# Finer pieces at the borders of stages, and in the running sums, of an eight-stage network on one core

## The reference

```python
S = jax.nn.relu(att[:, 0]); S = S.at[..., 0].set(0.0); S = S * (1.0 - eye)
FF = jnp.cumsum(shift_down_one_row(S), axis=1)       # running sum over the queries
att = att - FF[:, None]
keep = rank_of(FF_with_inf_above_diagonal) < eff_k   # about 409 keys per row, and the diagonal
y = softmax(where(keep, att, -inf)) @ v
```

## Time and profile before

| | |
|---|---|
| Time, 3 runs | 3022.83 us median (3011.96 to 3023.34) |
| The profiled execution | 3018.02 us, its span 3016.3 us, mean TensorE clock 0.946 |
| Busy, share of span | TensorE 88%, VectorE 63%, ScalarE 59%, GpSimd 11% |
| Running sums | 30.0 to 145.0 us |
| Attention of stage 1 | 400.3 to about 1010 us |
| Border 6 to 7: load issued, first product | 2755.97 and 2775.55 us |
| Border 7 to 8: output bias, first logit | 2825.15 and 2844.07 us |
| Load issued at the end, last instruction | 3001.87 and 3010.78 us |

### The profile page before, as it was taken

How to read it: one execution, slowest core, us unless ns; L and a number is a source line. 1 busy time by engine, 2 the same in 40 slices (tenths; PEclk the granted TensorE clock), 3 DMA queues, 4 the chain that set the end, 5 groups by cost and what they waited for, 6 DMA issues and landing times. The chain is left out here.

```text
span 3016.3 us, 75172 instructions
## 1 busy us (share of the span) xinstructions
PE 2657.2 (88%) x30828; PEld 1637.2 (54%) x30828; DVE 1889.0 (63%) x5219; ACT 1765.3 (59%) x3448; POOL 340.7 (11%) x709
## 2 busy tenths in 40 slices
PE   7898968888888799999998989999999999795386
PEld 3386955666666562212122546676666767463254
DVE  5399988878787573100001758878878787654762
ACT  2376846656666428999996246666666666421231
POOL 2100023222222010000000000000000000043025
PEclk9898989999999899999999999999999999897698
DMA  3250001111100102100000010000000000312003
GB/s 108 35 58 1 2 2 17 17 17 17 17 17 10 53 1 76 54 33 1 1 1 17 1 39 7 2 7 7 7 2 7 7 2 2 94 25 36 28 16 56
DMA packets 79982, 67.81 MB, mean 22 GB/s; under 512 B 40440, under 2 KB 67208, under 8 KB 79256
## 3 DMA queue, kind: packets, MB, share of 16 engines
q1 hardware_dynamic: 71192, 56.70, 8.1%
q0 software_dynamic: 8448, 6.30, 1.6%
HBM read 47.21 MB, written 19.96 MB: 22 GB/s over the span
## 5 line engine op out<-in xcount | busy, mean ns | idle before, releaser
L1711 ACT ACTIVATE arena<-ps 128x1024 f32<-128x1024 f32 x512 | 474.1, 1281 | 25.9 <-PE ps L1661 24.0
L1159 DVE CUSTOM_DVE_ANT_0 arena<-ps,arena 128x1024 f32<-128x1024 f32 (+7 forms) x384 | 350.1, 931 | 104.7 <-PE ps L1033 89.4
L2090 DVE CUSTOM_DVE_ANT_0 arena<-ps,arena 128x512 f32<-128x512 f32 (+3 forms) x640 | 373.0, 643 | 16.3 <-PE ps L1954 13.2
L1109 ACT ACTIVATE arena<-ps 128x1024 f32<-128x1024 f32 (+2 forms) x320 | 274.4, 895 | 125.0 <-PE ps L1066 121.5
L2044 ACT ACTIVATE arena<-arena 128x1152 f32<-128x1152 f32 (+15 forms) x256 | 306.0, 1200 | 60.2 <-DVE arena L2090 60.1
L1672 PE MATMUL ps<-arena 128*32 128x512 f32 x2048 | 273.0, 604 | 0.0
L1985 PE MATMUL ps<-arena 128*64 128x128 f32 x4352 | 268.8, 276 | 2.3 <-DVE arena L2105 1.5
L1954 PE MATMUL ps<-arena 64*128 64x512 f32 (+3 forms) x1280 | 266.0, 541 | 2.1 <-ACT arena L2020 1.1
L1985 PEld LDWEIGHTS ps<-arena 128*64 128x64 f32 x4352 | 234.7, 137 | 55.4 <-issue 45.7
L868 PE MATMUL ps<-arena 128*128 128x256 bf16 (+1 forms) x2176 | 238.1, 273 | 15.7 <-DVE arena L840 9.0
L1802 DVE COPY arena<-ps 128x512 f32<-128x512 f32 x16 | 11.1, 692 | 356.5 <-PE ps L1672 356.5
(11 more groups left out here) (294 smaller groups left out, 4159.6 us busy)
## 6 DMA issues: line engine op xcount, KB each, us to landing
arena<-scr_q SPq DMA_DIRECT2D x256, 32.0 KB
scr_s<-scr_f SPq DMA_DIRECT2D x1, 4096.0 KB, 16.9
arena<-scr_k SPq DMA_DIRECT2D x32, 128.0 KB
arena<-by_head_k SPq DMA_DIRECT2D x16, 192.0 KB
arena<-scr_s SPq DMA_DIRECT2D x16, 192.0 KB, 2.6
arena<-by_head_q SPq DMA_DIRECT2D x28, 96.0 KB
by_head_k<-arena SPq DMA_DIRECT2D x5, 512.0 KB, 4.4
scr_x<-arena SPq DMA_DIRECT2D x2, 1024.0 KB, 5.3
```

Source lines behind the costliest of these rows:

```text
L1109: e.activation(turned_block(u, kc), src, ACT.Exp, scale=-1.0).then_inc(exped, 1)
L1159: e.tensor_tensor_reduce(scored_block(u, g)[:, lo:hi], PS[:, 1024 * (k % 2):1024 * (k % 2) + hi - lo], NF[t][:, lo:hi], -1.0, mxs[:, col - ...
L1711: e.activation(PTR[k % RS], PS[:, at(n):at(n) + 1024], ACT.Sigmoid, scale=float(1 / np.sqrt(8.0))).then_inc(weighed, 1)
L2090: e.tensor_tensor_reduce(slot(u, t, g)[:, lo:hi], PS[:, base(step) + 512 * g:base(step) + 512 * g + hi - lo], bias, -1.0, mxs[:, col - 1:c ...
```

## The change

1. **Running sums.** Scores go two tiles ahead instead of one (a third `srow`), and piece by piece between the sums' pieces. The carry is added by pieces, right after each piece's sum, and a sum waits for its own piece's carry only. `cacc` is cleared by GpSimd at the start of the program. `X + bias`, `rpe_vector` and `split` move 2 or 3 tiles later. The third `srow` lies over `QS`, so SP's loads of queries wait for the last carry.
2. **Attention.** The first pair is (0, 7) instead of (7, 0). Three units of tile 0 go first, tile 7's penalty is made between them, and tile 0 stays three units ahead.
3. **Borders of stages 6, 7 and 8.** The reload of `X` goes in four DMAs with a semaphore each. In stage 6, `norm_moments` and `norm_rows` of stage 7's quarters 0 to 2 stand between the additions; in stage 7, likewise for stage 8. Stage 7's four output biases stand ahead of its additions. Logits come between the `norm_turn` of quarters. `wide(7)` and `weigh(7)` stand behind the last `down` and `scale`. The output goes in four DMAs.

```diff
+            order = [("score", n) for t in (0, 1) for n in pieces_of[t]]
+            for t in range(NT):
+                more = [("score", n) for n in pieces_of[t + 2]]
+                while len(more) > len(pieces_of[t]):
+                    order.append(more.pop(0))
+                for n in pieces_of[t]:
+                    if more:
+                        order.append(more.pop(0))
+                    order.append(("sum", n))
...
             def sums_scalar(e, w):
...
-                        if t >= 2:
-                            w.wait_ge(f_carry, t)
...
+                        if t >= 3:
+                            w.wait_ge(f_carry, upto[t - 3])
...
             def sums_vector(e, w):
-                e.memset(cacc, 0.0).then_inc(f_carry, 1)
-                for t in range(NT):
-                    W = 128 * (t + 1)
-                    w.wait_ge(f_summed, upto[t])
+                w.wait_ge(filled, 2)
+                for n, (t, c0, c1) in enumerate(chunks):
+                    w.wait_ge(f_summed, n + 1)
...
-            pairs = [(7, 0), (15, 1), (14, 2), (13, 3), (12, 4), (11, 5), (10, 6), (9, 8)]
+            pairs = [(0, 7), (15, 1), (14, 2), (13, 3), (12, 4), (11, 5), (10, 6), (9, 8)]
...
+            ahead = 3
+            units = [(0, p) for p in range(ahead)]
+            for p in range(8):
+                units += [(7, p)] + [(0, p + ahead)] * (p + ahead < 8)
+            units += [(t, p) for x in pairs[1:] for p in range(8) for t in x]
...
-                e.dma_start(by_tile(X), sum_rows.rearrange("(t p) c -> p t c", p=128)).then_inc(ec["d_back"], 16)
+                for c in range(4):
+                    e.dma_start(by_tile(cols(X, c)), sum_rows[512 * c:512 * c + 512].rearrange("(t p) c -> p t c", p=128)).then_inc(ec_back[c], 16)
...
                 for c in range(4):
+                    w.wait_ge(ec_back[c], 16 * (r + 1))
                     v = e.tensor_tensor(cols(X, c), cols(X, c), cols(SUM, c), ALU.add)
-                v.then_inc(x_ready, 1)
+                    if r == 0 and c < 3:
+                        norm_ahead(e, w, 6, c, 6, v)
+                        if c:
+                            norm_rows(e, w, 6, c - 1, ROWS7)
+                    elif r:
+                        v.then_inc(x_added, 1)
+                if r == 0:
+                    v.then_inc(x_ready, 1)
+                    norm_rows(e, w, 6, 2, ROWS7)
...
                     for c in range(4):
-                        w.wait_ge(ln_ht, 24 + max(c + 1, min(n, 3) + 1))
+                        if n == 3:
+                            norm_turn(e, w, 6, 3, HR, 3)
+                        w.wait_ge(ln_ht, 24 + c + 1)
...
-            e.dma_start(out.rearrange("b (t p) c -> p (b t) c", p=128), by_tile(X)).then_inc(d_out, 16)
-            w.wait_ge(d_out, 16)
+            for c in range(4):
+                w.wait_ge(x_added, 12 + c + 1)
+                e.dma_start(rows[:, 4 * c:4 * c + 4, :], by_tile(cols(X, c))).then_inc(d_out, 16)
+            w.wait_ge(d_out, 64)
```

More of the change, by code:

```diff
@@ L661, in qkv_vector @@
                 w.wait_ge(d_w, 64)
-                w.wait_ge(ones, 1)
+                w.wait_ge(filled, 1)
                 for n in range(12):
@@ L678, in qkv_gpsimd @@
             def qkv_gpsimd(e, w):
-                e.memset(V9, 1.0).then_inc(ones, 1)
+                e.memset(V9, 1.0).then_inc(filled, 1)
+                e.memset(cacc, 0.0).then_inc(filled, 1)
             cacc = reg(AT + 4096, 2048)
@@ L898, in stage1 @@
             extras = {}
+            for j in range(n_penalty[7]):
+                extras.setdefault((ahead * j // n_penalty[7], 1, 0), []).append((7, j))
             for k in range(1, 8):
@@ L901, in stage1 @@
                 for i, x in enumerate(steps):
-                    extras.setdefault((16 * (k - 1) + 15 * i // len(steps), 1, 0), []).append(x)
+                    first = ahead if k == 1 else 0
+                    extras.setdefault((16 * (k - 1) + first + (15 - first) * i // len(steps), 1, 0), []).append(x)
             plan = TileOrder(units, tiles, extras, space, {"score": -0.3, "shift": 0.1, "flip": -0.65, "add": -0.8, "turn": -0.15, "close": -0.3})
@@ L1136, in attend_vector @@
                 e.memset(SM[:, 256:320], 0.0).then_inc(fixed, 1)
-                for t in pairs[0]:
-                    for j in range(n_penalty[t]):
-                        penalty_vector(e, w, t, j)
+                penalty_vector(e, w, 0, 0)
                 for step in plan.steps:
@@ L1184, in attend_gpsimd @@
                 w.wait_ge(fixed, 6)
-                clear(e, w, pairs[0][0])
                 for step in plan.steps:
@@ L1232, in stage1 @@
             return {"sync": sync, "tensor": tensor, "vector": vector, "scalar": scalar, "gpsimd": gpsimd}
-        moe = {n: sem(f"m_{n}") for n in ("d_w", "logits", "scored", "routed", "made", "gated", "hidden", "spread", "turned", "scaled", "summed", "added")}
+        moe = {n: sem(f"m_{n}") for n in ("d_w", "logits", "scored", "routed", "made", "gated", "hidden", "spread", "turned", "scaled", "summed")}
         def stage_moe(r, stage, next_rows):
@@ L2290, in tensor @@
                         merge(x + 2)
-                    wide(x + 2)
+                    if x < 5:
+                        wide(x + 2)
                 down(5)
+                wide(7)
+                if r == 0:
+                    for c in range(3):
+                        norm_turn(e, w, 6, c, ROWS7, c)
             N_COPIED = 12
@@ L2561, in tensor @@
                     m.then_inc(mixed, 1)
+                for c in range(3):
+                    norm_turn(e, w, 7, c, ROWS8, 4 + c)
             def scalar(e, w):
                 w.wait_ge(x_ready, 6)
-                layernorm_scalar(e, w, 6)
+                norm_root(e, w, 6, 3)
+                norm_take(e, w, 6, 3, 3)
                 for i, m in enumerate((M, E)):
@@ L2617, in ended @@
         def ended(e, w):
-            w.wait_ge(x_ready, len(stages))
-            e.dma_start(out.rearrange("b (t p) c -> p (b t) c", p=128), by_tile(X)).then_inc(d_out, 16)
-            w.wait_ge(d_out, 16)
+            rows = out.rearrange("b (t p) c -> p (b t) c", p=128)
+            for c in range(4):
+                w.wait_ge(x_added, 12 + c + 1)
+                e.dma_start(rows[:, 4 * c:4 * c + 4, :], by_tile(cols(X, c))).then_inc(d_out, 16)
+            w.wait_ge(d_out, 64)
         block = ctx.enter_context(nc.Block())
```

130 lines of the change are left out of this document (77 added, 53 removed).

## The result

Median of 14 runs 3008.35 us (3000.14 to 3021.72), beside 3022.39 us (3011.8 to 3029.91) of the kernel before. The ratio is 0.9958, its 95% interval 0.9941 to 0.9975: 7.5 to 18 us gained, 12.7 in the middle. The forecast was 19.4 (3000 us). The profiled execution took 3005.58 us, its span 3003.8, which is 12.5 less than before.

The account below looks back on a forecast made before the run. TensorE was taken to bound the running sums, VectorE the attention's start, a DMA, VectorE and TensorE chain the borders. -10.8 - 2 + 1.3 - 2.7 - 1 - 4.2 = -19.4 on 3018.0 us: 2998.6, given as 3000; range 2987 to 3014.

Parts of the forecast that it names:

- Clock: Running sums: long 8-row score blocks lower TensorE's clock; with single pieces 16.9 us lost becomes 4.5, a gain of 12.4.
- The third rival: Running sums: single 8-row pieces between sums hold the clock at half through tiles 6 to 13; 3056 us, chance 0.06.
- Changes: Running sums: 63 instead of 29 changes between scores and sums on TensorE, 0.19 us each; 6.5 us lost.
- Idle: Running sums: TensorE's waits for the clear and carries shrink from 5 to 1.5 us, tile 3 still waiting; gain 3.5.
- Tail: After the last sum: only the last 512 columns' carry is left, some 0.7 us instead of 2.29; gain 1.4.
- Attention's start: First pair of the attention: tile 7's last three units run without a tile 0 unit and its wait; -2 us.
- Border 6|7: Stage 6 to 7: weights issued behind a later x_ready become the late wait, fourth norm_turn delays the fourth product; +1.3 us.
- Border 7|8: Stage 7 to 8: VectorE's layernorm ends 1.1 us earlier, two quarters of logits precede the last norm_turn; -2.7 us.
- 5|6: Stage 5 to 6: rows come no earlier, only the interleaving counts; -1 us.
- The end: Last reload of X and store of the output: load and store overlap by quarters; -4.2 us.
- the first rival: Running sums: the clock does not come back, its falls having another cause than score blocks; 3011 us, chance 0.25.
- this rule: Running sums: an always busy TensorE keeps its clock, so short scores bring nothing back; the sum lacks 12.4 us.

Follow-up runs that it names:

- e_before2: The kernel before, run once more with no edit: 3054.98 us, beside 3048.46 for the kernel before.
- e_oldsums: The changed kernel with the running sums of the kernel before (parts 2 and 3 of the change only): 3051.39 us, kernel before 3048.46.
- e_clear: The changed kernel, but GpSimd makes its clears without waiting for the constants at the start: 3002.63 us, kernel before 3013.88.
- e_oldatt: The changed kernel with the attention's old order, pair (7, 0) first and its penalties ahead of everything: 3009.34 us.
- e_wearly: The changed kernel, but SP loads stage 7's weights in the middle of stage 6, not after x_ready: 3036.50 us, kernel before 3048.46.
- e_wapart: The changed kernel, but stage 6's hidden products wait only for W1 and b1, not W2 and b2: 3029.89 us, kernel before 3048.46.
- f_after2: The changed kernel unchanged, run again on another chip: 3037.65 us (median of seven), ratio 0.9959 to the kernel before.
- e_blocks: The changed kernel, but all scores of a tile stand in one block ahead of a tile's sums: 3005.78 us, kernel before 3013.88.
- e_rows128: The kernel before, but its scores contract over all 128 rows instead of 8, so they sum all heads: 3002.29 us, kernel before 3013.88.
- f_zero: The changed kernel with GpSimd's early clears and scores over 128 rows, 120 of them zero: 3014.79 us (median of four), ratio 0.9872 to the kernel before.
- f_best: f_zero plus the edits of e_wearly and e_wapart: 2999.71 us (median of five), ratio 0.9826 to the kernel before.
- f_rows32: f_zero, but its scores contract over 32 of the 128 rows: 3014.12 us, kernel before 3059.24.
- runs 3, 8 and 10: e_rows128 (3002.29 us), f_zero (3014.79 us) and f_best (2999.71 us), all with scores over 128 rows.
- run 8: f_zero (3014.79 us), with f_after2 (3037.65 us) beside it on the same chip.
- runs 1 to 4: e_clear (3002.63 us), e_blocks (3005.78 us), e_rows128 (3002.29 us) and e_oldatt (3009.34 us).

## Why the prediction was right, and where not

The accounts of all executions of the running sums:

| kernel | work | low clock | idle |
|---|---|---|---|
| old order: before, `e_before2`, `e_oldsums` | 93.6, 93.4, 93.2 | 16.9, 13.9, 24.0 | 4.5 each |
| new order: after, `e_clear`, `e_oldatt`, `e_wearly`, `e_wapart`, `f_after2` | 99.3 to 100.2 | 1.7, 5.2, 12.0, 15.0, 10.2, 18.9 | 0.0 |
| new order in blocks: `e_blocks` | 92.9 | 10.4 | 0.0 |
| old order, 128 rows: `e_rows128` | 88.4 | 3.3 | 4.7 |
| new order, 128 rows: `f_zero`, `f_best` | 88.2, 88.2 | 0.0, 0.0 | 0.0 |
| new order, 32 rows: `f_rows32` | 100.2 | 0.0 | 0.0 |

- **Clock, the step that failed.** "I take long score blocks as the cause" and 12.4 us given back. Single 8-row pieces lower the clock too: in the mean the new order loses 10.5 us instead of the 4.5 that I left, and the old one 18.3. By these means the term is -7.8, not -12.4; but six executions between 1.7 and 18.9 and three between 13.9 and 24.0, on several chips, leave that difference open by about as much as it is. The length of the blocks is not the cause: `e_blocks`, with blocks of up to 2048 columns, lost 10.4. Weights on 8 rows are, in blocks or not; runs 3, 8 and 10 remove it. I took one execution's windows for the kernel's. The third rival (single pieces count as the blocks did) had the mechanism, but not its size: up to 20 us at a stretch ran at half clock (50 to 71 us in `e_oldatt`), not all of tiles 6 to 13.
- **Changes.** +6.5 foretold, 99.8 - 93.4 = +6.4 measured. Right, but I took it for a price of the order. It is one of unequal weights: 128-row scores pay nothing. And the interleaving bought nothing for it here: `e_blocks` has the same look-ahead, the same carries and no idle time either, and took 103.3 us from the first score to the last sum, against 101.9 to 118.2 with single pieces (mean 110.4).
- **Idle.** -3.5 foretold, -4.5 measured; tile 3 never waited. Tail: from the last sum's end to the first mask 4.8 us before and 3.4 now, the -1.4 foretold.
- The running sums together: -7.8 - 4.5 + 6.4 - 1.4 = -7.3 instead of -10.8, by the means. The first profile showed -14.5, a lucky draw.
- **Clearing `cacc` on GpSimd** I costed at nothing. It costs 0 to 1.9 us, since it can hold up one `TENSOR_SCALAR` of VectorE's layernorm at the one place where that is the chain.
- **Attention's start**, -2: the place behaved as said; the sum can't be told from scatter.
- **Border 6|7**, +1.3 foretold, +1.4 measured, by the wait named (weights issued behind the later `x_ready`). First product 18.9 after the reload, foretold 19.1.
- **Border 7|8**, -2.7 foretold, -2.3 measured. In all eleven executions of the new border, from the output products to the search of stage 8, it is 2.2 to 3.8. **5|6**, -1 foretold: the search began 2.2 earlier, more than I said, and nearly all of it was lost again behind the load of weights, which I had not looked at. The last count came 58.7 to 59.4 us after stage 5's end, before 59.1 to 59.4: 0.8 at most is left. At 7|8 VectorE's layernorm did not end 1.1 earlier (18.5 us after the first bias, 18.6 before); the logits alone gave the gain.
- **The end**, -4.2 foretold, -4.6 measured.
- By these terms: -7.3, +0.9 (the clear, in the mean), +1.4, -2.3, -4.6, 0 to -0.8 at 5|6 and 0 to -2 in the attention, together -12 to -15. The measured gain, 7.5 to 18, holds them; it can't say more.
- The time lies in the stated range, which reaches past the first rival, in which none of the clock comes back (a gain of 7.0). The measured 12.7 lies between that and the forecast's 19.4, and its interval holds neither. That the range held says little for the cause that I gave.
- Two slips in the prediction's sums: with no low clock at all the running sums give -15.3, not -16, and 3018 - 28 is 2990, not 2989. Nothing hangs on them.

In `f_after2` TensorE was busy for 20, 43 and 42 us of as many, and the granted clock was 0.83, 0.80 and 0.84; in `f_zero` it was as busy and had 1.00. The Trainium skill ("TensorE: Matmul & The Clock Gate", What's actually happening) ties the clock to how busy TensorE has been. By that rule alone the two would not differ; the measurement decides, and what differs between them in this stretch is the rows that the products fill, with zeros, and with it the 0.19 us at each change (which `f_rows32` pays at a clock of 1.00). In the prediction I had weighed this rule and kept it as a rival; it fell with run 8.

## What to carry to other kernels

Where the granted clock is below 1.00 beside a TensorE that is never idle, look at what the products fill: if weights have few rows, try to fill them up with zeros. Here a pass took the same 0.86 us so, and the change to and from full weights became free; the price was one clear on GpSimd and four copies on ScalarE. Profile the same kernel two or three times before a term of 10 us is read off the clock of one execution. Before a wait is costed as hidden, look at what the same queue waits for next: a load behind `x_ready`, a count behind a product, a clear beside the neighbour's layernorm. Measure a border at the first instruction whose time does not scatter: at 5|6 with the same waits the last count repeats within 0.8 us, the first scatter only within 8.4.

## What the runs showed of the hardware

- In a stretch with float32 products whose weights have 8 rows the granted clock fell to 0.50 (1.2 GHz) in ten executions of ten, 1.7 to 24.0 us lost in 102 to 122, in seven of them with TensorE busy without a pause. With 128 rows 0.0 of 88 us in two, and 3.3 in a third, all of it in two stretches that each follow a pause of 2.3 or 2.4 us.
- At each change between weights of 8 or 32 rows and weights of 128 rows a float32 product of 512 columns loses 0.19 us; between equal ones nothing (1.05 against 0.86).
- Beside clears on GpSimd a `TENSOR_SCALAR` of 128x4 on VectorE took 0.83 us instead of 0.17, until the clear was over, and 2.58 us, until the next clear was over too, in three executions of six.
- The kernel before took from 3014 to 3059 us on the chips of these runs. A good part of that lies where GpSimd gathers and scatters rows: from the search of stage 8 to its reload of `X` the kernels here took 150 to 152 us in the first profiles and in runs 1 to 4, and 160 to 167 on the three other chips.
